# First stage of a two-layer attention and expert kernel: a new order of TensorE's work within a step

## What is computed

```python
x = x + _L0_xattn_ref(ctx_1024, _layernorm(x), w_q, w_kv, w_out, b_out)   # 16 heads of 16
x = x + _L0_ffn_ref(_layernorm(x), gate_w, gate_b, expert_w, expert_b)    # counts of the two best of 8 experts
x = x + _L1_xattn_ref(_layernorm(x), ctx_1024, ctx_1024, mask)            # one head of 256
x = x + _L1_ffn_ref(_layernorm(x), W1, b1, W2, b2, Wg, bg)                # two of 8 experts per token
```

## Time and profile before

| | |
|---|---|
| median of three runs | 1204.52 us |
| profiled execution, its own time | 1202.87 us |
| its span in the profile | 1201.1 us |
| TensorE (PE) matmul busy | 998.3 us, 83% |
| VectorE (DVE) busy | 812.5 us, 68% |
| ScalarE (ACT) busy | 533.8 us, 44% |
| GpSimd (POOL) busy | 437.8 us, 36% |
| mean granted TensorE clock | 0.955 of full speed |
| first stage, first to last matmul of L437 | 52.0 to 548.1 us |

### The profile page before, as it was taken

One profiled execution on the slowest core, in us unless ns is written; L12 is line 12 of the kernel. 1 busy time (PEld: TensorE's weight loads), 2 busy tenths in 40 slices (PEclk: granted clock), 3 DMA queues, 4 the chain that ended last, 5 costly groups with the idle time before them and its releaser, 6 DMA issues. The chain is left out here.

```text
span 1201.1 us, 30730 instructions
## 1 busy us (share of the span) xinstructions
PE 998.3 (83%) x10536; PEld 706.0 (59%) x10536; DVE 812.5 (68%) x2319; ACT 533.8 (44%) x1055; POOL 437.8 (36%) x616
## 2 busy tenths in 40 slices
PE   3688889888888988876499999999986289999993
PEld 2366666666666666654255555555554168888872
DVE  4567777777777777764468888888887436666652
ACT  1365666565566666544113232233333045555551
POOL 4322222222222222200115555555556335555444
PEclk9999999999999999988599999999998579999997
DMA  4543333333333343210445555555554135555443
GB/s 126 148 123 117 105 114 112 110 107 114 118 104 117 101 120 105 86 38 2 128 133 166 151 150 150 152 153 150 151 156 133 50 106 89 101 92 94 86 63 36
DMA packets 104712, 133.93 MB, mean 112 GB/s; under 512 B 23806, under 2 KB 93902, under 8 KB 104398
## 3 DMA queue, kind: packets, MB, share of 16 engines
q1 hardware_dynamic: 91024, 113.86, 32.5%
q0 software_dynamic: 13536, 18.10, 8.8%
HBM read 93.78 MB, written 38.68 MB: 110 GB/s over the span
## 5 line engine op out<-in xcount | busy, mean ns | idle before, releaser
L612 DVE TENSOR_REDUCE smax<-psum 112x2 f32<-112x750 f32 x256 | 235.9, 933 | 120.6 <-PE psum L355 120.6
L526 ACT ACTIVATE probsT<-psum 125x896 f32<-125x896 f32 x192 | 175.9, 916 | 39.2 <-PE psum L370 39.2
L1454 POOL DMA_INDIRECT out_dram<-y,token_at x70 | 109.9, 1570 | 117.1 <-DMA out_dram<-y,token_at 61.0
L1535 ACT ACTIVATE h<-psum,b 128x256 f32<-128x256 f32 x140 | 58.8, 471 | 102.5 <-PE psum L1482 102.5
L296 POOL TENSOR_TENSOR ctx_lo<-ctxT,ctx_hi 128x750 f16<-128x750 f32 x32 | 51.7, 1614 | 133.1 <-ACT ctx_hi L533 133.1
L1011 POOL DMA_INDIRECT dispatch_dram<-rows,slots_at x64 | 64.0, 1000 | 94.1 <-DVE slots_at L1314 78.3
L1035 PE MATMUL psum<-xT_hi,we_hi 128*128 128x448 f16 x256 | 71.2, 360 | 26.2 <-DVE acc L1203 12.8
L390 PE MATMUL psum<-probsT,v_aug 125*32 125x112 f32 x3072 | 90.2, 267 | 0.0
L355 PE MATMUL psum<-k_stack,q_stack 63*128 63x375 f16 x512 | 84.9, 329 | 2.1 <-ACT xnT L566 1.3
L1203 DVE SCALAR_TENSOR_TENSOR acc<-psum,neg_bias,acc 128x448 f32<-128x448 f32 x112 | 75.7, 677 | 8.6 <-PE psum L1035 8.6
L370 PE MATMUL psum<-q_stack,k_stack 64*128 64x112 f16 x1536 | 70.3, 210 | 8.2 <-ACT probsT L526 6.8
(11 more groups left out here) (215 smaller groups left out, 2405.1 us busy)
## 6 DMA issues: line engine op xcount, KB each, us to landing
ctxT<-in_ctxT_dram SPq DMA_DIRECT2D x64, 375.0 KB, 4.2
k_stack<-k_hi_dram SPq DMA_DIRECT2D x64, 188.0 KB, 2.7
ctx_rows<-in_ctx_dram SPq DMA_DIRECT2D x32, 375.0 KB
rows_e<-dispatch_dram SPq DMA_DIRECT2D x70, 136.0 KB, 2.5
w_raw<-in_w_dram SPq DMA_DIRECT2D x32, 256.0 KB, 4.6
k_hi_dram<-k_hi SPq DMA_DIRECT2D x32, 188.0 KB, 1.9
k_lo_dram<-k_lo SPq DMA_DIRECT2D x32, 188.0 KB, 1.9
k_stack<-k_lo_dram SPq DMA_DIRECT2D x32, 188.0 KB, 2.8
```

What stands on the lines that cost most here:

```text
L526: nc.scalar.activation(probsT[:, p, c, hg, :, :, :].rearrange("p k h q -> p k (h q)"), psum[0:KC, 0:2, 0:4 * S], ACT.Exp, scale=float(HD) ...
L612: nc.vector.reduce_max(smax[:, (u - LAG_B) % 2, 2 * (s % 4) + s // 4::PAIRS], psum[0:S, pair_bank(s):pair_bank(s) + 2, 0:KV], AX.X).then_i ...
L1454: nc.gpsimd.indirect_dma_start(dram["out"], bass.IndirectOffsetOnAxis(token_at[:, n % 2, s:s + 1], 0), y[:, n % 2, s, :], None, compute_op ...
L1535: nc.scalar.activation(h[:, c, :], psum[:, 1 + c // 2, (c % 2) * TILE:(c % 2 + 1) * TILE], ACT.Relu, bias=b1[:, c, bass.ds(e, 1)]).then_in ...
```

## The change

On TensorE the transposes of xn come first and the transpose of the maxima after value groups 0 and 1 (in steps with part a). Since xn's transposes write bank 3, which pair 6 of the previous step used, they wait for maximum 6 (PAIRS - 1). The queries go ahead of scores 0. The gate stands between value groups 2 and 3 instead of ahead of both. keys(0) goes ahead of scoresT 0. The third values chunk goes to bank_d; it waits for the sum into x that read bank_d last (x1_ready), value group 0 of the next step waits for its copy, and the queries for the copy of chunks 0 and 1 alone. On ScalarE exps 5 and xnT come ahead of neg_max, and k_hi 0 ahead of exps 0. On VectorE xT_lo comes ahead of maximum 0. No operation is added or removed.

```diff
@@ -411,13 +411,16 @@
                 def vals(chunks):
                     if chunks[0] == 0:
                         wait(pe, m["klo_ready"], count(t, u, 2, 2))
+                    elif d:
+                        wait(pe, m["x1_ready"], count(t, u - LAG_D, 1, 1))
                     else:
-                        wait(pe, m["v_ready"], count(t, u, 2, 1))
+                        wait(pe, m["v_ready"], count(t, u - 1, 2, 2))
+                    bank = bank_a if chunks[0] == 0 else bank_d
...
-                                last = nc.tensor.matmul(bank_a[0:KC, n * D:(n + 1) * D], x[:, b2a, kc, cc * KC:(cc + 1) * KC], w[:, kc, :],
+                                last = nc.tensor.matmul(bank[0:KC, n * D:(n + 1) * D], x[:, b2a, kc, cc * KC:(cc + 1) * KC], w[:, kc, :],
...
                 if d:
                     scoresT(t, u - LAG_D, 5)
-                if c:
+                def turn_maxima():
+
                     wait(pe, m["max_done"], count(t, u - LAG_C, PAIRS, PAIRS))
                     nc.tensor.transpose(psum[0:H, 2, 0:S], smax[:, (u - LAG_C) % 2, :], ident[0:S, 0:S]).then_inc(m["mT_done"], 1)
+
+                if c and not a:
+                    turn_maxima()
                 if a:
                     wait(pe, m["xn_ready"], count(t, u, 1, 1))
+                    if c:
+                        wait(pe, m["max_done"], count(t, u - LAG_C, PAIRS, PAIRS - 1))
                     for kc in range(DC):
                         last = nc.tensor.transpose(psum[:, 3, kc * S:(kc + 1) * S], xn[:, kc * 128:(kc + 1) * 128], ident[0:S, 0:S])
                     last.then_inc(m["xnT_done"], 1)
                 if d:
                     wait(pe, m["x1_ready"], count(t, u - LAG_D - 1, 1, 1))
+                    wait(pe, m["v_ready"], at_most(count(t, u - 1, 2, 2), 2 * B))
                     values(0)
                     values(1)
+                if c and a:
+                    turn_maxima()
                 if e:
                     wait(pe, m["x1n_ready"], count(t, u - LAG_E, 1, 1))
...
-                pair_scores(0)
-                if a:
-                    wait(pe, m["v_ready"], count(t, u - 1, 2, 2))
+                if a:
+                    wait(pe, m["v_ready"], count(t, u - 1, 2, 1))
                     wait(pe, m["xnT_ready"], count(t, u, 1, 1))
...
                     last.then_inc(m["q_done"], 1)
+                pair_scores(0)
+                if d:
+                    values(2)
                 if e:
...
                 if d:
-                    values(2)
                     values(3)
                 pair_scores(1)
+                if a:
+                    keys(0)
                 unit_scoresT(0)
                 pair_scores(2)
-                if a:
-                    keys(0)
                 if d:
...
-                if c:
+                def negate_maxima():
+
                     wait(act, m["mT_done"], count(t, u - LAG_C, 1, 1))
                     wait(act, m["m_in"], count(t, u - LAG_C - 1, 32, 32))
                     nc.scalar.activation(neg_max[:, :], psum[0:H, 2, 0:S], ACT.Copy, scale=-1.0).then_inc(m["negm_ready"], 1)
+
+                if c and not a:
+                    negate_maxima()
+                if d:
+                    exps(t, u - LAG_D, 5)
                 if a:
                     wait(act, m["xnT_done"], count(t, u, 1, 1))
                     wait(act, m["q_done"], count(t, u - 1, 1, 1))
                     nc.scalar.activation(xnT[:, :, :].rearrange("p c s -> p (c s)"), psum[:, 3, 0:DC * S], ACT.Copy).then_inc(m["xnT_ready"], 1)
-                if d:
-                    exps(t, u - LAG_D, 5)
+                if c and a:
+                    negate_maxima()
...
+                if a:
+                    khi(0)
                 unit_exp(0)
-                if a:
-                    khi(0)
                 unit_exp(1)
...
-                pair_max(0)
                 if e:
                     wait(dve, m["x1hi_ready"], count(t, u - LAG_E, 1, 1))
                     nc.vector.tensor_tensor(xT_lo[:, :, bass.ds(be * S, S)], psum[:, 4, 0:DC * S].rearrange("p (c s) -> p c s", c=DC),
                                             xT_hi[:, :, bass.ds(be * S, S)], ALU.subtract).then_inc(m["x1lo_ready"], 1)
+                pair_max(0)
```

More of the change, by code:

```diff
@@ L551, in vout @@
                     nc.scalar.activation(v_aug[:, u % 4, chunks[0]:chunks[-1] + 1, :, 0:HD],
-                                         bank_a[0:KC, 0:len(chunks) * D].rearrange("p (n h w) -> p n h w", h=H, w=HD),
+                                         (bank_a if chunks[0] == 0 else bank_d)[0:KC, 0:len(chunks) * D].rearrange("p (n h w) -> p n h w", h=H, w=HD),
                                          ACT.Copy).then_inc(m["v_ready"], 1)
@@ L584, in step @@
                     nc.scalar.activation(oT[:, :, :].rearrange("p g s -> p (g s)"), bank_d[:, 0:4 * S], ACT.Copy).then_inc(m["oT_ready"], 1)
-                unit_exp(0)
                 if a:
                     khi(0)
+                unit_exp(0)
                 unit_exp(1)
```

## The result

The changed kernel took 1163.41 us (median of four runs, 1160.42 to 1166.43) against 1206.26 (four runs, 1202.75 to 1208.31): a ratio of 0.9656, 95% interval 0.9623 to 0.969. A second series gave 0.9688 (0.9641 to 0.9735). The forecast was 1171 in 1160 to 1186: right in sign and range, with a time 7.6 us too long. Between the medians the gain is 42.9 us, where 32.7 were forecast.

The account below looks back on a forecast made before the run. TensorE's order was taken to set the 16.20 us step, with waits for late items. 27 steps at 0.96 us (25.9), step 4 (0.5), start (2.2) and end (4.1) made 32.7 us; forecast 1171, range 1160 to 1186.

Parts of the forecast that it names:

- The path to keys(1): First part of a step, from scoresT 5: keys(1) at 8.86 us instead of 9.65, gaining 0.79 us.
- The turn ahead of scoresT 0: TensorE's extra change between full-array and half-array weights: between nothing and 0.26 us, taken as 0.1.
- The path from there to scoresT 5: Second part of a step, keys(1) to scoresT 5: 6.38 us instead of 6.55, a gain of 0.17.
- Maxima behind values: Head of a step: transpose of the maxima at 1.88 us instead of 1.20, removing its 0.84 us wait.
- The queries' place: Queries 0.28 us behind x1n's transposes, at 2.27 us, ahead of scores 0 at 3.35; no gain of their own stated.
- keys(0): Moved ahead of scoresT 0, it delays scores 2 and so k_lo 0: a cost of about half a microsecond a step.
- rival D: ScoresT 0 waits for the two DMAs of the maxima's row; at 6.3 us about 1210, slower; chance 0.03.
- The start: Steps 0 and 1 lose a 0.69 us wait each, steps 2 and 3 some 0.4 each: together 2.2 us.
- step 4: Has no gate, loses only the wait for maxima, less what the keys cost: 0.5 us, an estimate.
- The third chunk: Values chunk moved to bank_d: its 0.28 us wait for ScalarE's copy goes, with 1.0 us of cover.
- The end: Steps 32 and 33 lose a 1.41 us gate wait each, steps 34 and 35 gain 0.65 each: together 4.1 us.
- the clock's loss: Lower clock near step 32, counted as unchanged since other waits remain; if the clock holds, the total gain is 34 us.

Follow-up runs that it names:

- experiment 10: Kernel before plus only the gate's edits in steps without part a (values 2 ahead of the gate, xT_lo ahead of maximum 0): 1199.94 us, ratio 0.9955.
- experiment 5: Changed kernel with keys(0) back behind scores 2 on TensorE and k_hi 0 back behind exps 0 on ScalarE: 1159.58 us, ratio 0.9662.

## Why the prediction was right, point by point

- **The path to keys(1)**, the main mechanism, held almost item by item. Behind scoresT 5 I had scores 1 at 5.32 us (measured 266.61 - 261.30 = 5.31), scoresT 0 at 6.66 (6.64), scores 2 at 6.86 (6.85), scoresT 1 at 8.1 (8.09), keys(1) at 8.86 (8.74). The 0.12 is the term that was mis-sized: k_lo 0 follows maximum 2 by 0.93 instead of 1.02. On the way small errors cancelled: scores 0 came 0.13 sooner than reckoned (264.52) and the gate with values 3 took 0.06 longer. The turn ahead of scoresT 0 was priced at 0.1 by loose working (0.17 is the spacing of two neighbouring items, not a difference); keys(0) to scoresT 0 measured 1.07 where 1.08 was reckoned.
- **The path from there to scoresT 5**: 6.38 forecast, 15.13 - 8.74 = 6.39 measured, with scoresT 5 behind exps 4. Step 15.24 forecast, 15.13 measured; 25.9 us forecast for 27 steps, 28.4 and 28.6 measured.
- **Maxima behind values** as the main term: right, in both directions (17.5 alone, 20.9 undone).
- **The queries' place** had no term of its own in the sum; I let them ride with the maxima. Undone it costs 0.49 us a step, half of it the wait for neg_max and half unexplained. The parts overlap (20.9, 16.8, 4.4, 0.4 and -6.8 make 35.7), so the shares are not to be added as if they were separate.
- **keys(0)**: forecast to cost half a microsecond, costs 0.42. What I missed is the other side: rival D, the late row of maxima, was real in a few steps. The 4.18 us on which I argued against it is the one arrival that made scoresT 0 wait and so could be read. In a full step of the kernel before scoresT 0 stood 5.62 us behind the transpose (265.12 - 259.50) and did not wait, which only says that the row had landed by then. That 4.78 would be enough was not shown by these rows. In one step of the changed kernel it arrives 5.16 us behind the transpose (293.49 to 298.65), at a cost of 0.46:

```profile
298.65 0.37 PE L370 MATMUL psum<-q_stack,k_stack 64*128 64x112 f16 x8 [0.39 <-DMA q_stack<-neg_max]
```

- **The start** was forecast at 2.2 us and step 4 at 0.5. The two pairs give 0.3 and 2.0 together, and two profiles of one kernel reach step 5 3.3 and 5.0 us apart (79.8 and 83.1 changed, 80.1 and 85.1 before), so this term is not tested by them. The third chunk no longer waits, as these matmuls of step 0 show against the earlier trace rows. But in this profile it runs at 0.64 us a pair of matmuls instead of 0.43 (in the second one it returns to 0.38 within the chunk), and in both profiles steps 2 and 3 wait 1.27 us for q_lo ahead of keys(0), where step 2 waited 0.54 before. The forecast had left this wait out:

```profile
27.74 0.64 PE L423 MATMUL psum<-wv_hi,ctx_hi 128*125 128x256 f16 x2
...
44.27 0.48 PE L406 MATMUL psum<-ctx_hi,wk_hi 128*128 128x375 f16 x2 [1.27 <-DVE q_lo L693]
```

- **The end** was the term of the sum that was too small by the largest share: 4.1 forecast, 8.7 and 5.8 measured in the two pairs, 6.9 on average over all profiles (experiment 10). I counted the clock's loss as unchanged. By the rule of the Trainium skill, "TensorE: Matmul & The Clock Gate", "What's actually happening", activity releases the throttle; by that the full clock was to be kept where the wait was filled. The trace agrees for steps 32 and 33 of the first profile. In the changed kernel step 32 reads:

```profile
489.92 1.36 PE L390 MATMUL psum<-probsT,v_aug 125*32 125x112 f32 x48
491.21 0.41 PE L465 MATMUL psum<-ident,x1n 112*128 112x112 f32 x2
491.55 0.33 PE L355 MATMUL psum<-k_stack,q_stack 63*128 63x375 f16 x2
491.81 0.78 PE L390 MATMUL psum<-probsT,v_aug 125*32 125x112 f32 x24
492.52 0.27 PE L484 MATMUL psum<-gate_whi,xT_hi 128*112 128x8 f16 x2
```

Values 2 stand where TensorE idled 1.41 us, and the 24 matmuls take 0.78, what they take in full steps. But the reason I had given, that other waits remain, was right too: two steps on the clock falls again, behind a stretch in which TensorE is busy 2.30 of 4 us and its longest waits are 0.85 us, for ScalarE's probabilities.

```profile
514.31 2.03 PE L390 MATMUL psum<-probsT,v_aug 125*32 125x112 f32 x48
```

```profile
510.00:514.00 4.00, 2.30 (x34) 1.33 (x32) 3.85 (x7) 2.39 (x3) 0.53 (x2) 1.00 0.00 0
514.00:518.00 4.00, 4.00 (x83) 2.98 (x77) 0.83 (x3) 1.41 (x3) 0.26 (x1) 0.60 0.03 7
```

In the second profile of the same kernel it falls a step earlier, in step 33 (48 matmuls in 2.08 us at 505.32), and again in step 34. So part of the loss stayed and part came back, and which part differs from one execution to the next.

- **The total.** The terms of the first stage add up to 37.5 and 36.3 us where 32.7 were forecast. The rest of the measured gain is the last stage's 5.7 and 3.1 us, which no term had. Without them the time would still lie inside the range, some 3 to 6 us higher. (1170.2 and 1.65 make 1171.9; the forecast was written down as 1171.)

## What to carry to other kernels

When one engine's hand-written list sets the pace, walk one whole period with start-to-start distances from its own timeline and let every cross-engine latency compete; here this gave each of TensorE's items up to keys(1) within 0.15 us. Price a moved item at both ends: keys(0), moved ahead to come sooner, delayed the scores that its successor waited for, and yet bought slack for a DMA that is late only sometimes. The longest latency of a DMA that one trace happens to show is no bound for it.

## What was unexpected of the hardware

- Filling waits can save more than their length. In experiment 10 some 3.5 us of waits were filled and 9.2 us saved, as the granted clock stayed at 1.00 up to the last output projection. But the clock also fell behind shorter waits: in the changed kernel to an average of 0.60 from 514 to 518 us, with no idle time above 0.85 us in the four microseconds ahead, in step 34 of one profile and from step 33 on in the other.
- In experiment 5 scoresT 0 comes 3.5 us behind the maxima's transpose, and in 22 of 27 steps the two small DMAs have landed by then; in the other five they are up to 1.3 us late, four times without being issued late, and the late steps are largely the same in other kernels. The cause was not found.
- Splitting 48 f32 matmuls around six f16 ones lengthens the step by 0.14 us, with no wait to be seen in it. The six differ from the 48 in type and also in tile (128*112 against 125*32), and no run separates the two.
